# Places of the narrow diagonal tiles, banks of the tasks beside, and place of the output's split on POOL, in a four-layer hybrid block

## What is computed

```python
x = x + state_space(layernorm(x))     # scan over the tokens, gelu, layer norm
x = x + channel_mix(layernorm(x))
x = x + attention(layernorm(x))
x = x + channel_mix(layernorm(x))

# attention: 16 heads of 64 channels, keys and values by a latent of rank 128
latent = x @ w_kv_down; kv = latent @ w_kv_up
k, v = kv[..., :HD], kv[..., HD:]; q = x @ w_q
att = einsum('bqhd,bkhd->bhqk', q, k) * HEAD_SIZE ** -0.5
att = softmax(where(causal, att, -inf))
y = einsum('bhqk,bkhd->bqhd', att, v).reshape(Bx, Tx, HD) @ w_out
```

## Time and profile before

| | us |
|---|---|
| median of 3 runs | 2225.58 |
| lowest, highest | 2222.75, 2227.15 |
| the profiled execution | 2222.64 |
| its span, first to last instruction | 2221.3 |
| PE busy (matmuls) | 2004.8 |
| POOL busy | 1423.1 |
| DVE busy | 1323.7 |
| ACT busy | 1077.5 |

### The profile page before, as it was taken

The page is one execution under the profiler, slowest core; times in us unless marked ns, Lnnn a source line. Parts: engine busy times, 40 slices in busy tenths (PEclk is TensorE's granted clock), DMA queues, the critical chain, the costliest instruction groups (busy, mean ns, idle before and its releaser), DMA issues.

```text
span 2221.3 us, 33667 instructions
## 1 busy us (share of the span) xinstructions
PE 2004.8 (90%) x12886; PEld 1257.5 (57%) x12886; DVE 1323.7 (60%) x2728; ACT 1077.5 (49%) x1596; POOL 1423.1 (64%) x812
## 2 busy tenths in 40 slices
PE   8987688888999999999988998999899989998889
PEld 6765455545555655555555655555456555554566
DVE  7876655656666555555655556565656565655353
ACT  5775444434444444444454544444444444544575
POOL 1433235776777777777756686766677777777822
PEclk9999799999999999999998999999999999999999
DMA  3000000000000000000000000000000000000001
GB/s 118 1 1 1 0 7 13 17 13 9 18 12 18 9 18 12 18 10 18 12 18 9 11 19 11 17 11 19 11 17 11 19 10 17 11 13 11 25 24 57
DMA packets 29232, 36.90 MB, mean 17 GB/s; under 512 B 6928, under 2 KB 20368, under 8 KB 29072
## 3 DMA queue, kind: packets, MB, share of 16 engines
q1 hardware_dynamic: 29072, 34.76, 5.1%
HBM read 30.02 MB, written 4.46 MB: 16 GB/s over the span
## 4 chain that ended last, share of the span: by engine, by line
PE 54%; DVE 19%; ACT 11%; POOL 9%; issue 6%; DMA 1%; SPq 0%; ACTq 0%; POOLq 0%; DVEq 0%
PE heads_out L947 19%; PE scores L752 7%; PE two_heads L903 7%; POOL acc L1443 6%; PE beside L752 5%; ACT prob L1359 5%; DVE part_max L1141 4%; PE scores L926 3%; PE scores L932 3%; PE scores L930 3%; PE scores L928 3%; DVE two_heads L1138 2%; DVE stats L986 2%; PE two_heads L752 1%; PE beside L958 1%
## 5 line engine op out<-in xcount | busy, mean ns | idle before, releaser
L1443 POOL TENSOR_TENSOR acc<-acc,prob 128x1024 f32<-128x1024 f32 (+3 forms) x512 | 1015.5, 1983 | 236.0 <-ACT prob L1359 189.7
L1359 ACT ACTIVATE prob<-scores 128x1024 f32<-128x1024 f32 (+3 forms) x640 | 550.6, 896 | 632.9 <-PE scores L932 308.8
L1141 DVE TENSOR_REDUCE part_max<-two_heads 128x2 f32<-128x1024 f32 x384 | 468.4, 1220 | 324.7 <-PE two_heads L903 324.1
L947 PE MATMUL heads_out<-prob,V 128*64 128x512 f32 (+3 forms) x2560 | 531.9, 559 | 7.2 <-ACT prob L1359 7.0
L903 PE MATMUL two_heads<-k_hi,q_hi 64*128 64x512 f32 (+3 forms) x1280 | 284.6, 440 | 122.8 <-DVE part_max L1141 78.2
L1138 DVE CUSTOM_DVE_ANT_0 two_heads<-two_heads,mask 128x128 f32<-128x128 f32 (+3 forms) x512 | 241.1, 512 | 250.7 <-PE two_heads L903 250.6
L947 PEld LDWEIGHTS heads_out<-prob,V 128*64 128x64 f32 x2560 | 176.1, 142 | 319.0 <-issue 300.3
L926 PE MATMUL scores<-q_hi,k_hi 64*128 64x512 f32 (+3 forms) x1280 | 246.0, 379 | 30.5 <-ACT prob L1359 17.4
L903 PEld LDWEIGHTS two_heads<-k_hi,q_hi 64*128 64x128 f32 x1280 | 121.2, 185 | 262.6 <-DVE part_max L1141 110.8
L930 PE MATMUL scores<-q_lo,k_hi 64*128 64x512 f32 (+3 forms) x1280 | 236.6, 363 | 0.0
L932 PE MATMUL scores<-neg_max,sel 64*128 64x512 f32 (+3 forms) x1280 | 236.6, 363 | 0.0
(11 more groups left out here) (295 smaller groups left out, 2884.1 us busy)
## 6 DMA issues: line engine op xcount, KB each, us to landing
rden<-rden_rows SPq DMA_DIRECT2D x128, 128.0 KB, 2.9
X<-u SPq DMA_DIRECT2D x8, 512.0 KB, 8.9
out<-X SPq DMA_DIRECT2D x8, 512.0 KB, 2.9
wQK_raw<-wQuery SPq DMA_DIRECT2D x16, 192.0 KB, 3.1
wO_raw<-wOut SPq DMA_DIRECT2D x16, 128.0 KB, 2.8
wV_raw<-wValue SPq DMA_DIRECT2D x8, 128.0 KB, 2.7
den<-den_rows SPq DMA_DIRECT2D x64, 4.0 KB
rden_rows<-den SPq DMA_DIRECT2D x64, 4.0 KB, 1.3
```

The lines of the kernel that those rows point to most:

```text
L947: made = pe.matmul(heads_out[head(h), x0:], V[vn % NVS][:, tt, p % 2, head(h)], prob[step % NPROB][:, h, x0:], start=t == 0, stop=t == TPB ...
L1141: made = ve.reduce_max(part_max[:, t, :, c:c + 1], pair_of(task)[:, :, 0:width], AX.X)
L1359: ac.activation(prob[step % NPROB][:, :, x0:], scores[:, first:first + 2, x0:], ACT.Exp).then_inc(empty(task)[0], 1)
L1443: po.tensor_tensor(total[:, :, x0:], total[:, :, x0:], new[:, :, x0:], ALU.add).then_inc(acc_ok, 1)
```

## The change

Three edits, in the planner alone; no instruction is added to or taken from TensorE, DVE, ACT or SP, and POOL's have other widths in the units with j = 0.

- `TILE`: seven of the twelve diagonal tiles narrower than 512 columns now stand at a step with number 1 modulo 4, where one stood before. The tile of 128 columns is no longer a unit's last step.
- `SIDE`: the tasks beside are chosen by kind. First a project in bank 0; then a query, key, latent or turn_tiles in bank 7; then a value, turn_max or project in bank 1; each as soon as it is open. A fourth of any kind follows if it is due within four steps, in a bank that is not taken.
- "two_parts" goes behind the third product with V and add of a group in place of the second.

```diff
-SIDE = [7, 0, 1, 7]
-TILE = [[0, 1, 2, 3], [0, 1, 4, 5, 2, 3, 6, 7], [0, 1, 2, 8, 3, 4, 5, 9, 6, 7, 10, 11], [0, 1, 2, 12, 3, 4, 5, 13, 6, 7, 8, 14, 9, 10, 11, 15]]
+SIDE = [([0], ("project",), 99), ([7], ("query", "key", "latent", "turn_tiles"), 99), ([1], ("value", "turn_max", "project"), 99), ([0, 1, 7], None, 4)]
+TILE = [[0, 3, 1, 2], [0, 1, 4, 5, 2, 7, 3, 6], [0, 1, 2, 8, 3, 11, 4, 9, 5, 10, 6, 7], [0, 1, 2, 12, 3, 15, 4, 5, 6, 14, 7, 8, 9, 13, 10, 11]]
...
-        def filler(latest):
-            open_ = sorted((x for x in fillers if x[0] <= s and x[2] not in self.done and early(x[2])), key=lambda x: x[1])
+        def filler(latest, kinds=None):
+            open_ = sorted((x for x in fillers if x[0] <= s and x[2] not in self.done and early(x[2]) and (not kinds or x[2][0] in kinds)), key=lambda x: x[1])
             if open_ and open_[0][1] <= latest:
                 fillers.remove(open_[0])
                 self.need(*open_[0][2])
+                return True
...
-                    if (idx, t) == steps[s + 1]:
+                    if (idx, t) == steps[s + 2]:
                         due("two_parts")
...
-            for n, self.side_bank in enumerate(SIDE):
-                filler((10 ** 6, s + 16, s + 8, s + 4)[n])
+            taken = set()
+            for banks, kinds, ahead_by in SIDE:
+                self.side_bank = next((x for x in banks if x not in taken), 7)
+                if filler(s + ahead_by, kinds):
+                    taken.add(self.side_bank)
```

## The result

The changed kernel takes 2,187.2 us in the median (2,186.0 to 2,191.7), the kernel before on the same chip 2,226.4 (2,222.8 to 2,229.1): a ratio of 0.983, 95% interval 0.981 to 0.985. It is 1.7% faster. The profiled execution took 2,186.0, its span is 2,184.6 us; before it was 2,221.3. These 36.7 us are what the following accounts for.

What follows compares the result with a forecast made beforehand. TensorE's work, with its idle time and low clock, was taken to bound the kernel. 52 − 47 − 15 = −10 us against the profiled 2,222.6 gave 2,212.6, or 2,215 as a median, range 2,193 to 2,243.

Steps and rivals of the forecast that it cites:

- What bounds the kernel: Middle, 500 to 2,100 us: TensorE's work sets the end; only its 127 us idle and low-clock stretches can change.
- The new wait: Before each group's tasks beside: first task in bank 0 or 1 waits for score 0's exponential; 3.5 us a pair, 52 lost.
- I take it in full: Tasks beside: no later wait shrinks with the added one, so all 52 us count as lost.
- The narrow tiles: Scores before a group's last row maximum: fuller ones cover DVE's queue; 3.15 us a pair, 47 us gained.
- place 28: Group whose first product with V is number 28 of a head pair's 40 steps: last maximum's wait 2.1 to 1.2, gain 0.95.
- wO takes 1.1 to 1.7: DVE's split of wO before the group's third maximum (C) is reduced: 1.1 to 1.7 us, putting the fourth (D) at C + 3.4.
- Output split later on POOL: oT_lo behind one more POOL add: fills POOL's 4.39 us idle, priced at 0.
- no one gains: POOL's later output split: its adds are in time for exponentials, and the project needing oT_lo came 13 us later; worth 0.
- The clock: TensorE's 64 us at 1.2 GHz in the middle cost 32; half is gained, 15 us, bounds 0 and 30.
- two long waits in three to go: Waits over 1.5 us at a group's last maximum fall from about three in two pairs of heads to one.
- The clock and D give more: Faster rival: low-clock stretches nearly vanish (30 us), waits at groups' last maximum give 5 more; 2,195 us, chance 0.15.
- The new wait stays and its return doesn't come: Slower rival: 52 us lost before tasks beside, half of the 47 not gained, low clock unchanged; 2,240 to 2,253, chance 0.25.

Runs made afterwards that it cites:

- bank7_first: Changed kernel with another SIDE: first task beside always in bank 7, a query, key, latent or turn_tiles ahead of the project; 2,142.6 us.
- tile_and_side: Changed kernel without its third edit (two_parts back behind the second product with V and add); 2,216.5 us.
- parts_alone: Kernel before with only two_parts moved behind the third product with V and add; 2,223.6 us, ratio 1.000 to 1.004.
- tile_and_parts: Kernel before with the new TILE and the later two_parts, SIDE as before; 2,158.4 us.
- pieces_alone: Kernel before with each of POOL's 128x1024 adds issued as four of 256 columns; 2,211.1 us, ratio 0.995 to 0.999.
- tile_alone: Kernel before with the new TILE only; 2,164.4 us, ratio 0.970 to 0.978.
- side_alone: Kernel before with the new SIDE and filler only; 2,251.6 us, ratio 1.010 to 1.017.
- adds_in_pieces: tile_and_side with POOL's adds issued as pieces of 256 columns, each unit's first add left whole; 2,195.5 us.

## Why the prediction was wrong in size

**What bounds the kernel** held: TensorE's idle time and its clock were what could be won, and both moved as a sum of small waits.

**The new wait (52 us)** was right in place and nearly in size. Time lost in front of the first task, as means of even and odd pairs: 0.76 us at place 12 (forecast 0.8), 0.48 at 28 (0.6), 1.19 at 36 (1.25), 0.38 at 32 (0.35), 0.24 at 4 (0.35), 0.10 at 20 (0.1) and 0.05 at 0 (0.05): 3.2 us a pair, 48 in all. The step behind it, "I take it in full", is right only in part: at places 28 and 32 bank7_first takes the wait away and gets little or nothing back, and its 45 us hold gains from another order of tasks too. That its 2.9 us a pair lie near the 3.5 is partly luck.

**The narrow tiles (47 us)** were right at 0, 4, 8, 12, 16, 20, 24 and 36 to 0.2 us, and 0.23 short at 32. A step that failed is place 28: "wO takes 1.1 to 1.7", where it took 0.73 (median 0.71), so that D stood at C + 2.6 and not 3.4; the whole place came out 0.87 us a pair better than forecast. I had the range of the durations before and took its upper part as a property of the instruction; it is a property of the moment, POOL's remainder plus 0.28. The rule of the Trainium skill that I weighed there (GPSIMD Engine Reference, Specifications) says only that the two contend, and I drew from it that the split would stay long because POOL is busy before and after. The runs show that busy is not enough to say: with POOL at 65% the split takes 0.4 or 2.5 us by when it starts.

**Output split later on POOL (0)** is the term that failed, and place 28 is where it shows. The miss is 28 us, and this edit, priced at 0, measured 29. The text argued that "no one gains", since the exponentials and the project that need POOL are in time. It asked who waits for POOL by a semaphore, and not who is held by POOL without one. tile_and_side against the changed kernel puts 29 us on it, 34 in the profiled executions: about 1.5 us a pair at place 28, 22 in all, and 24 us of half clock, at half, 12. Without this edit the other two come to −3 us (2,219.1 to 2,216.5), where the forecast had −10; that this is so near is luck, since the end of the attention, which it left out, made up for a split of wO that was longer (2.2 us) than it had assumed. Without SIDE and TILE it is worth 0 (parts_alone), with TILE 6 (tile_and_parts), with bank7_first's banks 25. There is no price of this edit by itself; there are only phases.

**The clock (15 us)** had the right sign and, in the middle, the right size: of the 41 us less at half clock, 34 stand in ordinary pairs and at the change of batch, and give 17. Over the whole span it gave 26. I expected two long waits in three to go, and pieces_alone shows such a fall, in its fastest execution, without moving anything on TensorE. That low clock follows long waits is what parts_alone and pieces_alone point to, not more.

**The end of the attention (not in the sum)** gave 11 us, 7 of them by the clock. The forecast worked through ten places of a pair and multiplied; the last unit has other neighbours on DVE, and I had not read it. The **change of batch** went the other way: 7 us lost there beside the clock, with tile_alone gaining 1.5. SIDE is the cause: beside the clock, side_alone loses 7 us there against the kernel before and tile_and_side 7 against tile_alone, and bank7_first gets 5.6 of it back. Which wait it is, I didn't take apart.

**The rivals.** "The clock and D give more", 2,195, was the nearest, with its "5 us more at D" too small by far. "The new wait stays and its return doesn't come" describes side_alone (2,251.6, forecast 2,240 to 2,253), that is the second edit without the first.

## What to carry to other kernels

Price an edit by who waits for the moved work through a semaphore, and then by who shares a port with it: where DVE works from SBUF to SBUF beside a busy POOL, look up how much of POOL's instruction was left in every instance, for a duration with several levels in the trace is a wait in disguise. When a schedule repeats, read its last repetition apart from the rest. Change the parts of a mixed edit one by one: here `TILE` alone won 55 us, `SIDE` alone cost 33, and another `SIDE` on top of the change won 45.

## What the runs showed of the hardware

A DVE subtraction of 128x256 with two SBUF operands took 0.35 to 0.43 us with POOL idle, and else the running POOL instruction's remainder plus 0.280 to 0.289 us, in 158 of 158 cases with over 0.14 us left. With one operand in PSUM, DVE's instructions of 512 columns took 0.67 to 0.70 us whether POOL ran or not. Cutting POOL's add of 1,024 columns (2.38 us) into four of 256 (0.74 each) cost 24% more POOL time, and brought wO's split to at most 0.92 us in adds_in_pieces and 1.01 in pieces_alone. One of the latter began 45 ns before the end of a piece and took 1.01 us all the same, which is the next piece's length more.

Before 300 us all fourteen kernels run nearly the same instructions, yet their time at half clock from 0 to 300 us was 44.4 in seven of them and 51 to 61 in others. Executions of one kernel differ as well: the kernel before took 2,210.4 to 2,229.7 in 19 runs, pieces_alone 2,203.9 to 2,219.7 in 10, bank7_first 2,138.6 to 2,145.6 in 4. What decides in a given execution whether such a wait is followed by a stretch of low clock stays open.
